# A transformer tile kernel: the expert gate moved from a broadcast before the square to a per-token weight after the expert

## The reference

```python
x = x + tanh(g_xattn) * xattn(layernorm(x), ctx)       # 16 heads, 77 context tokens
z = layernorm(x)                                       # (4096, 128)
logits = z @ w_router                                  # 8 experts
top_vals, top_idx = top_k(logits, 2)
probs = softmax(top_vals)
h = square(relu(einsum('nc,ecd->ned', z, w1)))         # every expert, every token
y_all = einsum('ned,edc->nec', h, w2)
y_sel = take_along_axis(y_all, top_idx)
x = x + tanh(g_ffn) * sum(y_sel * probs)
```

## Time and profile before

| what | us |
|---|---|
| median of 3 runs | 412.71 |
| lowest and highest of the 3 | 410.66, 418.45 |
| the profiled execution | 408.92 |
| its span, first to last instruction | 407.1 |
| TensorE busy | 332.2 (82%) |
| VectorE busy | 228.4 (56%) |
| ScalarE busy | 169.6 (42%) |
| GpSimd busy | 112.7 (28%) |

### The profile page before, as it was taken

One profiled execution on the slowest core, in us unless ns is written; L12 is line 12 of the kernel. 1 busy time (PEld: TensorE's weight loads), 2 busy tenths in 40 slices (PEclk: granted clock), 3 DMA queues, 4 the chain that ended last, 5 costly groups with the idle time before them and its releaser, 6 DMA issues.

```text
span 407.1 us, 7987 instructions
## 1 busy us (share of the span) xinstructions
PE 332.2 (82%) x2728; PEld 255.1 (63%) x2728; DVE 228.4 (56%) x899; ACT 169.6 (42%) x394; POOL 112.7 (28%) x194
## 2 busy tenths in 40 slices
PE   0503788995999989989997999979998998996193
PEld 0302465663777867767776778757786885785183
DVE  5426453554566766666666566676667665336122
ACT  1200233441445545544553446455654653352111
POOL 8491403141403250415041322332313102002000
PEclk9955555565579978995899669998998998599578
DMA  3076191019141943291619151936182400600500
GB/s 91 4 116 141 38 133 28 4 33 140 36 185 33 146 107 161 47 143 34 209 36 141 33 190 49 138 61 217 37 122 82 158 3 21 217 2 1 203 32 26
DMA packets 17671, 36.62 MB, mean 90 GB/s; under 512 B 4633, under 2 KB 9370, under 8 KB 17632
## 3 DMA queue, kind: packets, MB, share of 16 engines
q1 hardware_dynamic: 13664, 27.29, 28.0%
q0 software_dynamic: 3680, 8.82, 11.1%
q10 hardware_dynamic: 288, 0.00, 0.0%
HBM read 23.14 MB, written 2.23 MB: 62 GB/s over the span
## 4 chain that ended last, share of the span: by engine, by line
PE 57%; DMA 14%; DVE 10%; issue 5%; SPq 4%; POOL 3%; ACT 2%; POOLq 0%; DVEq 0%; ACTq 0%
PE y L498 11%; PE c L449 9%; PE s L429 7%; DMA x_sb<-in_x_dram 7%; PE ab L407 6%; PE h L489 4%; PE h L490 3%; PE h L491 3%; SPq L274 3%; DMA qs<-mT 2%; PE ab L473 2%; PE ab L466 2%; POOL ks L1065 2%; PE c L460 2%; DMA qs<-q_lo 2%
## 5 line engine op out<-in xcount | busy, mean ns | idle before, releaser
L790 DVE TENSOR_REDUCE negm<-ab 128x4 f32<-128x308 f32 x128 | 59.4, 476 | 66.3 <-PE ab L407 65.1
L651 ACT ACTIVATE p<-s 77x512 f32<-77x512 f32 x128 | 74.4, 584 | 28.3 <-PE s L429 28.0
L498 PE MATMUL y<-w2s,hs 128*128 128x128 f32 x512 | 72.6, 289 | 8.6 <-ACT hs L658 8.5
L429 PEld LDWEIGHTS s<-qs,ks 104*77 104x77 f32 x512 | 67.6, 185 | 13.3 <-issue 6.8
L407 PE MATMUL ab<-ks,qs 96*128 96x312 f32 x128 | 59.8, 472 | 18.4 <-DMA qs<-q_lo 14.0
L498 PEld LDWEIGHTS y<-w2s,hs 128*128 128x128 f32 x512 | 66.7, 203 | 10.2 <-ACT hs L658 9.6
L429 PE MATMUL s<-qs,ks 104*77 104x128 f32 x512 | 70.7, 272 | 0.6 <-DMA qs<-mT 0.6
L658 ACT ACTIVATE hs<-u 128x512 f32<-128x512 f32 x64 | 40.1, 628 | 49.1 <-DVE u L904 46.6
L449 PE MATMUL c<-p,vs 77*32 77x128 f32 x1024 | 58.4, 327 | 0.0
L904 DVE SCALAR_TENSOR_TENSOR u<-h,gb 128x512 f32<-128x512 f32 x64 | 43.3, 681 | 23.6 <-PE h L491 11.6
L1034 POOL TENSOR_SCALAR rs<-mv 128x1 f32<-128x1 f32 x32 | 8.3, 258 | 143.2 <-DVE mv L831 143.1
(11 more groups left out here) (99 smaller groups left out, 453.9 us busy)
## 6 DMA issues: line engine op xcount, KB each, us to landing
gb<-gates_scratch SPq DMA_DIRECT2D x16, 768.0 KB, 5.8
qs<-q_hi SPq DMA_DIRECT2D x16, 256.0 KB, 7.1
gb<-gates_scratch SPq DMA_DIRECT2D x8, 512.0 KB, 4.0
ks<-k_hi SPq DMA_DIRECT2D x64, 39.0 KB
qs<-q_lo SPq DMA_DIRECT2D x8, 256.0 KB, 9.1
x_res<-in_x_dram POOLq DMA_DIRECT2D x8, 256.0 KB, 8.9
out_dram<-y_out POOLq DMA_DIRECT2D x8, 256.0 KB, 3.2
x_sb<-in_x_dram POOLq DMA_DIRECT2D x6, 256.0 KB, 7.4
```

The source lines that it names most:

```text
L429: mm = nc.tensor.matmul(p[0:N, T * i:T * i + T], ks[:, par, c, i, NP * j:NP * j + N], qs[:, par, c, T * j:T * j + T], start=True, stop=True)
L498: mm = nc.tensor.matmul(bank_y[:, D * b:D * b + D], hs[:, e % 2, T * b:T * b + T], w2s[:, e, :], start=(e == 0 and b == 0), stop=(e == E - ...
L651: nc.scalar.activation(p32[:, c, :], src, ACT.Exp).then_inc(p_done, 1)
L790: nc.vector.tensor_reduce(negm[:, :, c], bank_ab[bank][:, 0:J * NP].rearrange("t (i n) -> t i n", n=NP)[:, :, 0:N], AX.X, ALU.max, negate= ...
```

## The change

1. ACT does the positive part (`relu_square`: Relu from PSUM into u, then Square into hs); DVE's `gated` is gone, and with it gb and its three loads, the store to DRAM, `gates_turn`, `gate_rows`, POOL's `gate_roots` and one of the two exponentials of the gate.
2. The gates are no longer roots. DVE takes the reciprocal of the denominator itself, and the gates stay as they are, tokens on partitions.
3. `output` no longer adds up in PSUM: each expert overwrites bank y, and DVE's `weighed` reads it with four instructions of 128x128, one per sequence, out = y * gate + (x1 or the sum so far). `finish` is gone.
4. So expert e+1 may be written only when expert e has been weighed. In the last tile alone four banks are used in turn (y, c and the two s2).
5. `weighed` of e1 stands at the end of the DVE slot, behind `normalise2` (before it in the last tile). On TensorE `output` of e0 now stands ahead of `hidden` of e2.

```diff
 AB_USES = [
...
-    (-1, "turn3"), (0, "s1c3"), (-1, "route3"), (0, "s1d3"), (1, "v"), (0, "mT3"), (-1, "gates"),
+    (-1, "turn3"), (0, "s1c3"), (-1, "route3"), (0, "s1d3"), (1, "v"), (0, "mT3"),
...
             def output(s, par, e):
                 pe.wait_ge(hs_done, E * s + e + 1)
-                if e == 0 and s > 0:
+                back = 4 if last(s) else 1
+                if e >= back:
+                    pe.wait_ge(y_weighed, (E - 1) * s + e - back + 1)
+                elif e == 0 and s > 0:
                     pe.wait_ge(y_added, s)
...
+                p = weigh_bank(s, e)
                 for b in range(G):
-                    mm = nc.tensor.matmul(bank_y[:, D * b:D * b + D], hs[:, e % 2, T * b:T * b + T], w2s[:, e, :],
-                                          start=(e == 0 and b == 0), stop=(e == E - 1), skip_group_check=True)
+                    mm = nc.tensor.matmul(p[:, D * b:D * b + D], hs[:, e % 2, T * b:T * b + T], w2s[:, e, :],
+                                          start=True, stop=True)
...
+                    if e[0] is not None:
+                        output(sf, pf, e[0])
                     if e[2] is not None:
                         hidden(sf, pf, e[2])
                     if near[0]:
                         scoresT(*near[0], 3)
-                    if e[0] is not None:
-                        output(sf, pf, e[0])
-                    if j == 1 and exists(i - 1):
-                        gates_turn(i - 1)
...
-            def square(s, e):
+            def relu_square(s, e):
                 n = E * s + e
-                act.wait_ge(u_done, n + 1)
+                act.wait_ge(h_ready, n + 1)
+                if n >= 2:
+                    act.wait_ge(hs_done, n - 1)
+                nc.scalar.activation(u[:, e % 2, :], bank_h[e % 2][:, :], ACT.Relu).then_inc(relu_done, 1)
+                act.wait_ge(relu_done, n + 1)
                 if n >= 2:
                     act.wait_ge(y_done, n - 1)
                 nc.scalar.activation(hs[:, e % 2, :], u[:, e % 2, :], ACT.Square).then_inc(hs_done, 1)
...
+                dve.wait_ge(gate_d, at(GATE, s, "den"))
+                nc.vector.reciprocal(gt[:, 4, :], gt[:, 3, :]).then_inc(den_inverted, 1)
...
-                nc.vector.scalar_tensor_tensor(out=u[:, e % 2, :], in0=bank_h[e % 2][:, :], scalar=0.0,
-                                               in1=gb[:, par, e, :], op0=ALU.max, op1=ALU.mult).then_inc(u_done, 1)
...
+            def weighed(s, par, e):
+                p = weigh_bank(s, e)
+                dve.wait_ge(y_done, E * s + e + 1)
...
+                for b in range(G):
+                    ins = nc.vector.scalar_tensor_tensor(out=y_out[:, par, b, :], in0=p[:, D * b:D * b + D],
+                                                         scalar=gates[:, e, b:b + 1],
+                                                         in1=(x1 if e == 0 else y_out)[:, par, b, :],
+                                                         op0=ALU.mult, op1=ALU.add)
+                ins.then_inc(y_weighed if e < E - 1 else y_added, 1)
...
-                    if j == 1 and exists(i - 2):
-                        finish(sf, pf)
+                    if pending is not None and exists(sf):
+                        weighed(sf, pf, pending)
...
                     if near[-1]:
                         normalise2(*near[-1])
                     take(prepare, 9)
+                    if e[1] is not None and not last(sf):
+                        weighed(sf, pf, e[1])
```

More of the change, by code:

```diff
@@ L45, in ab_order @@
 def ab_order(step, tiles):
-    return [name for shift, name in AB_USES if 0 <= step + shift < tiles]
+    return [name for shift, name in AB_USES
+            if 0 <= step + shift < tiles]
 STATS = ["ctx_stats", "x_stats", "ctx_moments", "x_moments"]
@@ L254, in exists, with last, weigh_bank @@
             return 0 <= t < S
+        def last(t):
+            return t == S - 1
+        def weigh_bank(s, e):
+            return (bank_y, bank_c, bank_s2[0], bank_s2[1])[e % 4] if last(s) else bank_y
         @block.sync
@@ L593, in max_store @@
                                      ACT.Copy).then_inc(ab_taken[bank], 1)
-            def gate_rows(s):
-                bank, k = ab(s, "gates")
-                act.wait_ge(ab_ready[bank], k)
-                nc.scalar.activation(gatesT[:, :], bank_ab[bank][0:G * E, 0:T], ACT.Copy).then_inc(ab_taken[bank], 1)
             def evacuate_k(s, par):
@@ L662, in gate_exp @@
                 nc.scalar.activation(gt[:, 1, :], gt[:, 0, :], ACT.Exp).then_inc(gate_e, 1)
-                nc.scalar.activation(gt[:, 2, :], gt[:, 0, :], ACT.Exp, scale=0.5).then_inc(gate_e, 1)
             for dst, src in ((col(NG), norm_g.rearrange("(n o) -> n o", o=1)),
@@ L688, in step @@
                     if e[0] is not None:
-                        square(sf, e[0])
+                        relu_square(sf, e[0])
                     if near[2]:
@@ L694, in step @@
                     if e[1] is not None:
-                        square(sf, e[1])
+                        relu_square(sf, e[1])
                     if j == 3 and third:
@@ L702, in step @@
                     if e[2] is not None:
-                        square(sf, e[2])
-                    if j == 1 and exists(i - 1):
-                        gate_rows(i - 1)
+                        relu_square(sf, e[2])
                     if j == 2 and third:
@@ L996, in step @@
                     take(post)
-                    if e[1] is not None:
-                        gated(sf, pf, e[1])
+                    if e[0] is not None:
+                        weighed(sf, pf, e[0])
                     take(prepare)
-                    if e[2] is not None:
-                        gated(sf, pf, e[2])
+                    if e[1] is not None and last(sf):
+                        weighed(sf, pf, e[1])
                     take(prepare)
```

74 lines of the change are left out of this document (18 added, 56 removed).

## The result

The changed kernel takes 423.56 us (median of 4, 422.48 to 427.99), the kernel before in the same comparison 411.69 (4, 409.09 to 418.45). The ratio is 1.0331, with a 95% interval of 1.0224 to 1.0437: slower. Ratios leave out executions more than 1.5% above the fastest of the same kernel. The profiled execution has a span of 421.8 us at a mean granted clock of 0.812 (0.800 before). A second comparison of the same two kernels, on another occasion, gave 1.0166 (1.01 to 1.0233), slower again but by less than the 1.02 to 1.045 that I had expected of it, because there the kernel before took 417.35 us and the changed one 423.34.

What follows compares the result with a forecast made beforehand. TensorE was taken as the bound most of the time, waiting on VectorE at slot ends. Losses of 18.8 us less 6.1 gained at the end make 12.7, on a base of 412.71 forecasting 425 us, range 409 to 437.

Steps and rivals of the forecast that it cites:

- Price of a weighing: Four 128-element VectorE instructions per expert output: 1.1 us, replacing a gating of 0.68.
- Slot 3: Slot end: e1's weighing delays the first row maximum, so TensorE stands 1.1 us before `turn`; 6.6 us lost in 6 steps.
- Slot 2: Slot end: the weighing delays `transpose_x`, 0.95 us on average with part hidden at 1.2 GHz; 5.7 us lost in 6 steps.
- Slot 0: Slot end: 3.3 us lost in three steps without the late load of x, 0.9 in three with it.
- Slot 1: VectorE already bounds here: losing the gates' wait gains nothing, longer weighing and a reciprocal cost; 1.2 us lost in sum.
- Last full step: Its slot 3 and the end behind have fewer products to hide a weighing between two outputs: 1.1 us lost.
- The end: Last tile: hidden goes on at once with four banks while VectorE makes the gates; 6.1 us gained.
- ScalarE at zero: ScalarE's 64 added instructions, 40 us in 400, counted as no cost in the middle.
- GpSimd's transfers: Low-key transfers wait for the last `scoresT`, 0.82 us before them, not q_lo; that product moves 0.86 us later.
- The waits really go: Rival: slot 1's gates' waits are gained, slot ends cost nothing, low-clock stretches shorten; 15 us gained, 397 us; chance 0.18.
- Half hidden: Rival: each slot end costs only about 0.5 us; 3 us lost in all, 416 us; chance 0.24.
- The gaps bring the clock down: Rival: TensorE's gaps put four more slots at 1.2 GHz, about 2 us each; 433 us; chance 0.14.

Runs made afterwards that it cites:

- experiment 2: Changed kernel with one 512-element instruction per weighing instead of four of 128, using the first sequence's gate for all: 421.74 us, ratio 1.0101 to the kernel before.
- experiment 1: Changed kernel with expert 1's weighing moved behind the next slot's first row maximum on VectorE: 423.59 us, ratio 1.0183 to the kernel before.
- experiment 3: Kernel before, with TensorE transposing the earlier-ready sorted logits in place of the gates, removing the gates' wait: 406.22 us, ratio 0.9827.
- experiment 5: Load of x issued ahead of the low-key transfers: changed kernel 410.82 us (ratio 0.9753), kernel before 396.78 us (0.9525), the latter repeated at 401.26 us.
- experiment 6: Changed kernel, load of x first, weighings carried later: e1's, 400.78 us; expert 7's too, 401.74; both, with the pending output moved, 396.86.
- experiment 4: Changed kernel with one bank instead of four for the last tile's outputs: 429.29 us, ratio 1.0263 to the kernel before.

## Why the prediction came out right

Forecast 425.0, range 409 to 437; measured 423.56. Step by step:

- **What bounds.** Right: TensorE nearly everywhere, VectorE's order at the slot ends.
- **Price of a weighing, 1.1 us.** Right: 1.12 to 1.13 for four in a row in the timelines. The Trainium skill's "VectorE: DVE Perf Modes" gave estimates of 1.03 for four and 0.66 for one of 512 elements by its PSUM formula; the runs show 1.13 and 0.746, and these decide. Its advice, that many small tiles pay the fixed cost each time, is borne out: 0.38 us at each place (experiment 2).
- **Slot 3.** 6.6 predicted, 6.5 measured. The wait before `turn` is 0.98 us. It vanishes when that one weighing stands behind the maximum (experiment 1), and shrinks by as much as the weighing does (experiment 2): the cause of this wait is shown, not only argued.
- **Slot 2.** The 5.7 were 8.2. The mechanism is the one stated (a wait of up to 1.2 us before `transpose_x`), the difference is one slot at the lower clock, 3.9 us. Without it the term is 4.3, in five slots, for the 4.75 of five times 0.95.
- **Slot 0.** 4.2 predicted, 6.5 measured. The term for the three steps with the late load (0.9) was too small: they cost 1.71, 0.03 and 0.92, 2.7 together. The three others cost 1.57, 1.16 and 1.12, for which I had 1.1 each.
- **Slot 1.** 1.2 predicted, 2.3 measured, but not for the reason given. 2.1 of it come from step 5 alone (7.81 to 9.95 us), where the granted clock was 1.00 before and 0.57 after; the five others add up to 0.2. The reasoning was partly wrong: with the gates' wait taken out alone, the middle of the kernel before gains up to 2.3 us, not nothing (experiment 3). In the changed kernel that wait is gone too; that the longer VectorE chain takes the gain back is argued, not shown.
- **Last full step.** Slot 3 cost 0.9 for 1.1. Slot 2 of that step, for which I had nothing, took 7.91 us for 10.37, at a granted clock of 0.70 for 0.50.
- **The end.** 6.1 of gain predicted, 6.0 measured from slot 0 of step 8 on. Within it, the start of hidden was not at about the same distance: the last `turn` to the end gives 7.6, slot 0 of step 8 takes 1.5 back (7.17 to 8.72). ScalarE is waited for 0.46 to 0.66 us at the outputs there, five of them, as stated.
- **ScalarE at zero.** Right in the middle: 0.5 us of waits in 225.
- **GpSimd's transfers.** Right: they start 0.82 us behind the last `scoresT` (263.70 to 264.52), before q_lo has ended (264.56). The profile now names the product itself.

**The rivals.** "The waits really go" is refuted by 24.2 us of waits on negm. "Half hidden" is refuted by the 0.98, which comes back before every `turn` that ends a slot 3 in steps 1 to 5 (0.97 to 0.98), and by the 1.1 to 1.2 before `transpose_x`. "The gaps bring the clock down" isn't borne out as it was sized: the mean granted clock is 0.812 for 0.800 before. The slots that start at 311.33, 321.60, 339.34 and 349.59, each behind a wait of 0.98 us, ran at 1.00, and the one at 359.84 at 0.87 (0.86 before); those that start at 151.99 and 329.86, behind 0.96, ran at 0.84 and 0.82, where the same slots of the kernel before had 0.71 and 0.80. The lower clock of the middle steps stands behind the gaps of 2.4 to 3.1 us of slot 0 in steps 3 to 5 (188 to 208, 236 to 250 and 280 to 294 us). Part of this rival is in the result nevertheless, some 4 us in slot 2 and 2 in slot 1. The prediction's reading that the trace before agrees for waits of 1.4 us and more was too broad: behind the 1.73 us of the earlier trace rows the slot from 265.74 to 273.54 ran at 1.00.

That the sum is as near as it is owes something to luck, since terms offset each other: slots 0 to 2 were short by 5.9 us in all, and the start and step 7, for which I had 1.1 of loss, gave 3.9 of it back. On the profiled executions it is 14.6 (408.92 to 423.56) for 12.7. The base of 412.71 was also 1 us above the median of the comparison.

**What stays open.** Why a given gap of TensorE is followed by a lower clock in one run and not in another (1.49 us: no; 1.60, with 0.73 more right behind it: yes in experiment 1; 1.36: no in experiment 5; 1.20 and 1.44 at 395 and 398 us of the changed kernel: no, 1.00 from 372.4 to 416.7), and so which slots of a variant are slow. It moved slots by 1 to 4 us and probably hides in the total what experiments 1 and 2 show in the slots. Nor is it shown why slot 0 keeps 1.05 us in experiment 6, where the visible waits are 0.6. Whether a second bank for the outputs in the middle would turn the moved weighings into a gain wasn't tried: all banks are in use there.

## What to carry to other kernels

An instruction put ahead of a short one in an in-order queue costs the bound engine nearly its whole length (0.98 of 1.13 us here) if the short one is what that engine needs next, though the queue's engine is busy only 59%; look at the slot end, not at the share of busy time. Moving it behind gains only if nothing else waits for it: here the output's bank did, and the score products, and k_lo. And before working on the arithmetic, look at what stands ahead of each load in its queue: issuing one load earlier took 4.7% off the kernel before, more than the whole change put on it.

## What had not been expected of the hardware

- **A load behind a waiting transfer.** The load of x costs GpSimd 0.80 us to issue and stood behind a wait on TensorE and 2.29 us of other issues. Issued first, it removed TensorE's waits of 1.7 to 2.3 us in the middle and one of 4.47 near the start: 394.56 to 398.4 us against 414.34 to 419.15 in the same comparison.
- **Clock.** Slots at a granted clock of 0.53 to 0.57 took up to 3.6 us more than at 1.00 (11.84 against 8.25 us, experiment 1). Gaps of 1 us in nearly every slot didn't lower the mean granted clock: 0.812 for 0.800 before.
- **A releaser that the profile named wrongly.** Before, it named q_lo for the low-key transfers; after, with q_lo later, it named `scoresT`, and the distance to that was 0.82 us both times. A distance that stays the same was better evidence here than the name.
- **Four banks instead of one are worth 4.6 us in eight experts** at the end, where nothing else fills TensorE (experiment 4).
